# A gated recurrent layer on one core: six product groups of 64 columns become five, one of them 128 columns wide

## The reference

```python
def step(h, x_t):
    fused = sigmoid(concatenate([x_t, h], axis=-1) @ w_W + w_b)      # 1024 -> 1024
    hidden_state, output_state = split(fused, 2, axis=-1)            # r and z below
    memory_state = x_t @ wx_W + wx_b + hidden_state * (h @ wh_W + wh_b)
    h_new = output_state * h + (1.0 - output_state) * tanh(memory_state)
    return h_new, h_new
out = x + swapaxes(scan(step, h0, swapaxes(x, 0, 1))[1], 0, 1)
```

## Time and profile before

| | |
|---|---|
| time, median of 3 runs | 1796.21 us (1795.36 to 1796.39) |
| the profiled execution | 1795.32 us, of which its span is 1793.5 us |
| PE busy | 1766.1 us, 98% of the span |
| PEld busy | 1694.7 us, 94% |
| DVE busy | 1131.5 us, 63% |
| ACT busy | 789.8 us, 44% |
| POOL busy | 357.1 us, 20% |
| DMA | 29.9% of the 16 engines' span, mean 89 GB/s |

### The profile page before, as it was taken

How to read it: one execution, slowest core, us unless ns; L and a number is a source line. 1 busy time by engine, 2 the same in 40 slices (tenths; PEclk the granted TensorE clock), 3 DMA queues, 4 the chain that set the end, 5 groups by cost and what they waited for, 6 DMA issues and landing times.

```text
span 1793.5 us, 244402 instructions
## 1 busy us (share of the span) xinstructions
PE 1766.1 (98%) x110976; PEld 1694.7 (94%) x110976; DVE 1131.5 (63%) x7177; ACT 789.8 (44%) x3983; POOL 357.1 (20%) x1540
## 2 busy tenths in 40 slices
PE   6999999999999999999999999999999999999998
PEld 5899999999999999999999999999999999999997
DVE  2566666666666666666666666666666666666665
ACT  2444444444444444444444444444444444444443
POOL 0122222222222222222222222222222222222221
PEclk9999999999999999999999999999999999999999
DMA  6223332233332233322233322333222333223332
GB/s 215 59 87 92 92 92 76 75 92 94 93 91 72 79 92 92 93 76 81 87 92 92 92 70 80 96 92 92 82 75 85 93 95 93 73 78 91 92 92 82
DMA packets 180732, 159.89 MB, mean 89 GB/s; under 512 B 12016, under 2 KB 179440, under 8 KB 180720
## 3 DMA queue, kind: packets, MB, share of 16 engines
q1 hardware_dynamic: 180720, 159.72, 29.9%
HBM read 151.28 MB, written 8.39 MB: 89 GB/s over the span
## 4 chain that ended last, share of the span: by engine, by line
PE 97%; DMA 1%; SPq 1%; issue 0%; DVE 0%; ACT 0%; POOL 0%; POOLq 0%; DVEq 0%
PE ps L239 79%; PE ps L200 19%; DMA x_next<-in_x 1%; DMA x_sb<-in_x 0%; SPq L149 0%; SPq L158 0%; SPq L155 0%; DVE h L365 0%; SPq L146 0%; ACT h L304 0%; ACT h_by L299 0%; SPq L162 0%; SPq L153 0%; SPq L152 0%; SPq L151 0%
## 5 line engine op out<-in xcount | busy, mean ns | idle before, releaser
L239 PE MATMUL ps<-wh,h 128*8 128x64 f32 x98304 | 1504.4, 219 | 9.0 <-issue 5.1
L239 PEld LDWEIGHTS ps<-wh,h 128*8 128x8 f32 x98304 | 1390.9, 90 | 78.7 <-issue 6.7
L343 DVE STREAM_TRANSPOSE turned<-ps 128x64 f32<-128x64 f32 x3072 | 705.3, 239 | 402.6 <-PE ps L239 309.1
L295 ACT ACTIVATE m_by<-pre_r 128x16 f32<-128x16 f32 x1024 | 223.2, 218 | 548.5 <-DVE pre_r L346 548.4
L200 PE MATMUL ps<-x_next,wx_step 128*32 128x128 f32 x12288 | 430.2, 273 | 1.1 <-issue 1.1
L365 DVE TENSOR_TENSOR_SCAN h<-h_by,h 128x48 f32<-128x48 f32 x1024 | 264.0, 258 | 245.0 <-ACT h_by L299 192.1
L424 POOL TENSOR_TENSOR add<-turned,bias_h 128x16 f32<-128x16 f32 x1024 | 222.8, 218 | 714.8 <-DVE turned L343 684.3
L304 ACT ACTIVATE h<-m_pre 128x32 f32<-128x32 f32 x1024 | 237.7, 232 | 205.2 <-DVE m_pre L356 205.2
L299 ACT ACTIVATE h_by<-pre_z 128x16 f32<-128x16 f32 x1024 | 222.4, 217 | 220.6 <-DVE pre_z L350 220.6
L200 PEld LDWEIGHTS ps<-x_next,wx_step 128*32 128x32 f32 x12288 | 316.5, 110 | 1.4 <-issue 1.3
L437 POOL TENSOR_TENSOR y<-x_sb,h 128x32 f32 x512 | 134.1, 262 | 714.2 <-DVE h L365 714.2
(11 more groups left out here) (8 smaller groups left out, 1.1 us busy)
## 6 DMA issues: line engine op xcount, KB each, us to landing
wx_step<-in_w_x SPq DMA_DIRECT2D x516, 192.0 KB, 2.4
x_next<-in_x SPq DMA_DIRECT2D x132, 256.0 KB, 3.2
x_sb<-in_x SPq DMA_DIRECT2D x34, 256.0 KB, 3.2
out_h<-y SPq DMA_DIRECT2D x32, 256.0 KB, 2.7
...
bias_x<-in_b_x SPq DMA_DIRECT2D x1, 6.0 KB, 3.2
bias_h<-in_b_h SPq DMA_DIRECT2D x1, 2.0 KB, 3.0
```

The costliest lines, as they stand in the source:

```text
L239: mm = pe.matmul(ps[Q * j:Q * j + B, bank, 0:GROUP], h_of(s - 1, k), wh[:, k, j, at:at + GROUP], start=(start and k % HC == 0), stop=(not ...
L295: act.activation(m_by[:, o, :, 1], pre_r[:, o, :], ACT.Sigmoid).then_inc(r_ready[o], 1)
L343: return dve.transpose(turned[:, o, g], ps[:, GATES * o + g, 0:GROUP].rearrange("p (c q) -> p c q", q=Q))
```

## The change

Half B's R and M become one group, RM_B, of 128 columns in one bank. Its weights lie side by side already (R_B's 64 columns, then M_B's), so no array moves. A group is now a tuple of first column, number of columns and bank, and there are five: R_A, M_A, Z_A, RM_B, Z_B.

```diff
@@ constants
-    GROUP_BANKS = HALVES * GATES
-    X_BANKS = [GROUP_BANKS, GROUP_BANKS + 1, GROUP_BANKS]
+    R_A = (0, GROUP, 0)
+    M_A = (GROUP, GROUP, 1)
+    Z_A = (2 * GROUP, GROUP, 2)
+    RM_B = (3 * GROUP, 2 * GROUP, 3)
+    Z_B = (5 * GROUP, GROUP, 4)
+    GROUP_BANKS = 5
+    X_BANKS = [5, 6, 7]
@@ PE, x products
-                        if u == 0:
-                            pe.wait_ge(xg_free[2], free)
-                        elif u == 1:
-                            pe.wait_ge(xg_free[1], free)
-                        else:
-                            pe.wait_ge(xg_free[0], again)
+                        pe.wait_ge(xg_free[u], free)
@@ PE, h products
-            def products(o, g, half, s, start):
-                bank = GATES * o + g
-                at = GROUP * bank
+            def products(group, half, s, start):
+                at, cols, bank = group
                 for k in range(half * HC, (half + 1) * HC):
                     for j in range(TILES):
-                        mm = pe.matmul(ps[Q * j:Q * j + B, bank, 0:GROUP], h_of(s - 1, k),
-                                       wh[:, k, j, at:at + GROUP], start=(start and k % HC == 0),
+                        mm = pe.matmul(ps[Q * j:Q * j + B, bank, 0:cols], h_of(s - 1, k),
+                                       wh[:, k, j, at:at + cols], start=(start and k % HC == 0),
                                        stop=(not start and k % HC == HC - 1), tile_position=(0, Q * j))
@@ PE, step
                 pe.wait_ge(h_ready[0], nxt)
-                products(0, R, 0, s, True)
-                products(0, M, 0, s, True)
-                products(0, Z, 0, s, True)
-                products(1, M, 0, s, True)
+                products(RM_B, 0, s, True)
+                products(R_A, 0, s, True)
+                products(M_A, 0, s, True)
+                products(Z_A, 0, s, True)
                 pe.wait_ge(h_ready[1], nxt)
-                products(0, R, 1, s, False).then_inc(r_done[0], 1)
-                products(0, M, 1, s, False).then_inc(m_done[0], 1)
-                products(0, Z, 1, s, False).then_inc(z_done[0], 1)
-                products(1, R, 0, s, True)
-                products(1, R, 1, s, False).then_inc(r_done[1], 1)
-                products(1, M, 1, s, False).then_inc(m_done[1], 1)
-                products(1, Z, 0, s, True)
-                products(1, Z, 1, s, False).then_inc(z_done[1], 1)
+                products(R_A, 1, s, False).then_inc(r_a_done, 1)
+                products(M_A, 1, s, False).then_inc(m_a_done, 1)
+                products(Z_A, 1, s, False).then_inc(z_a_done, 1)
+                products(RM_B, 1, s, False).then_inc(rm_b_done, 1)
+                products(Z_B, 0, s, True)
+                products(Z_B, 1, s, False).then_inc(z_b_done, 1)
@@ ACT, step
                 reset(1, nxt)
+                update(1, nxt)
                 new(1, s, nxt)
-                update(1, nxt)
@@ DVE, turn
-            def turn(o, g):
-                return dve.transpose(turned[:, o, g], ps[:, GATES * o + g, 0:GROUP].rearrange("p (c q) -> p c q", q=Q))
+            def turn(group, o, g0, g1):
+                at, cols, bank = group
+                return dve.transpose(turned[:, o, g0:g1].rearrange("p g c q -> p (g c) q"),
+                                     ps[:, bank, 0:cols].rearrange("p (c q) -> p c q", q=Q))
@@ DVE, step, behind sum_r(0); what stands there in full is shown below
-                turn(1, R).then_inc(r_turned[1], 1)
-                turn(1, M).then_inc(m_turned[1], 1)
+                turn(RM_B, 1, R, Z).then_inc(rm_b_turned, 1)
@@ POOL, hidden
-                pool.wait_ge(m_turned[o], nxt)
+                pool.wait_ge(rm_b_turned if o else m_a_turned, nxt)
```

More of the change, by code:

```diff
@@ L110, in build @@
         constants = sem("constants")
-        r_done = halves("r_done")
-        m_done = halves("m_done")
-        z_done = halves("z_done")
-        r_turned = halves("r_turned")
-        m_turned = halves("m_turned")
-        z_turned = halves("z_turned")
+        r_a_done = sem("r_a_done")
+        m_a_done = sem("m_a_done")
+        z_a_done = sem("z_a_done")
+        rm_b_done = sem("rm_b_done")
+        z_b_done = sem("z_b_done")
+        r_a_turned = sem("r_a_turned")
+        m_a_turned = sem("m_a_turned")
+        z_a_turned = sem("z_a_turned")
+        rm_b_turned = sem("rm_b_turned")
+        z_b_turned = sem("z_b_turned")
         x_product = sem("x_product")
@@ L207, in first_x_products @@
                 for u, k in x_list:
-                    if k == 0 and u >= X_UNITS - 1:
-                        last = max(v for v in range(u) if X_BANKS[v % X_UNITS] == X_BANKS[u % X_UNITS])
-                        pe.wait_ge(xg_free[last % X_UNITS], last // X_UNITS + 1)
+                    if k == 0 and u >= X_UNITS:
+                        pe.wait_ge(xg_free[u % X_UNITS], u // X_UNITS)
                     if k == 0 and u * WX_PARTS % UNITS == 0:
@@ L213, in first_x_products, with x_products @@
                     x_product_of(u, k, wx[:, u, k, :], x_sb[:, k, 0:TOK])
-            def x_products(loaded, free, again, s):
+            def x_products(loaded, free, s):
                 pe.wait_ge(wx_step_loaded[s], loaded)
@@ L277, in _ @@
                     step(i, t0, s)
-                    x_products(loaded, free, again, s)
+                    x_products(loaded, free, s)
         @block.scalar
@@ L371, in step @@
                 par = s % 2
-                dve.wait_ge(r_done[0], nxt)
+                dve.wait_ge(r_a_done, nxt)
                 if s % RING == 0:
                     dve.wait_ge(y_added, held(dve, t0 + (s + STEPS)))
-                turn(0, R).then_inc(r_turned[0], 1)
-                dve.wait_ge(m_done[0], nxt)
-                turn(0, M).then_inc(m_turned[0], 1)
+                turn(R_A, 0, R, M).then_inc(r_a_turned, 1)
+                dve.wait_ge(m_a_done, nxt)
+                turn(M_A, 0, M, Z).then_inc(m_a_turned, 1)
                 dve.wait_ge(x_placed, nxt)
-                dve.wait_ge(r_turned[0], nxt)
+                dve.wait_ge(r_a_turned, nxt)
                 sum_r(0, par, nxt)
-                dve.wait_ge(z_done[0], nxt)
-                turn(0, Z).then_inc(z_turned[0], 1)
-                dve.wait_ge(r_done[1], nxt)
-                turn(1, R).then_inc(r_turned[1], 1)
-                dve.wait_ge(z_turned[0], nxt)
+                dve.wait_ge(z_a_done, nxt)
+                turn(Z_A, 0, Z, GATES).then_inc(z_a_turned, 1)
+                dve.wait_ge(z_a_turned, nxt)
                 sum_z(0, par, nxt)
                 mix_m(0, par, nxt)
-                dve.wait_ge(m_done[1], nxt)
-                turn(1, M).then_inc(m_turned[1], 1)
-                dve.wait_ge(r_turned[1], nxt)
+                dve.wait_ge(rm_b_done, nxt)
+                turn(RM_B, 1, R, Z).then_inc(rm_b_turned, 1)
+                mix_h(0, s, nxt)
+                dve.wait_ge(rm_b_turned, nxt)
                 sum_r(1, par, nxt)
-                mix_h(0, s, nxt)
-                dve.wait_ge(z_done[1], nxt)
-                turn(1, Z).then_inc(z_turned[1], 1)
+                dve.wait_ge(z_b_done, nxt)
+                turn(Z_B, 1, Z, GATES).then_inc(z_b_turned, 1)
+                dve.wait_ge(z_b_turned, nxt)
+                sum_z(1, par, nxt)
                 mix_m(1, par, nxt)
-                dve.wait_ge(z_turned[1], nxt)
-                sum_z(1, par, nxt)
                 mix_h(1, s, nxt)
```

5 lines of the change are left out of this document (2 added, 3 removed).

## The result

| | before | after |
|---|---|---|
| median | 1796.3 us | 1778.62 us (1777.43 to 1780.79, 4 runs) |
| ratio | | 0.9904, 95% interval 0.9887 to 0.9921 |
| profiled execution, span | 1795.32, 1793.5 us | 1779.06, 1777.2 us |
| step in the stage 300 to 1700 us | 3.415 us | 3.390 us |

The change gains 17.7 us. I had forecast 1751 us and a range of 1746 to 1775: the direction is right, but only two fifths of the gain came, and the time lies outside the range.

The account below looks back on a forecast made before the run. PE was taken as the bound, with one late start a step: 3.415 - 0.021 (fewer passes) - 0.068 (late start) = 3.326 us a step; 512 x 0.089 = 45.4 us, so 1796.21 becomes 1751, 8-in-10 range 1746 to 1775.

Parts of the forecast that it names:

- What bounds it: PE's own time sets the end; its one break, at the wait for `h_ready[1]`, costs 0.068 us a step.
- Part 1: On PE, 16 passes of 64 columns become 8 of 128, saving 0.021 us a step, 10.6 us in all.
- Part 2: More PE work ahead of `h_ready[1]` gives half B 0.213 us more, removing the 0.068 lateness: 34.8 us.
- part 3: Chains behind PE on DVE, ACT and POOL: both states arrive in time, with 0.03 (half A) and 0.02 us (half B) spare.
- deadline of 2.15: Half A's state must be written by 2.15 us after the first pass behind `h_ready[1]`; forecast at 2.12.
- the joint turn: RM_B's single turn on DVE ahead of half A's `mix_h`: may hold DVE 0.38 us, bounds 0.17 to 0.34, costs nothing.
- rival 1: State late again by 0.02 to 0.07 us: 1761 to 1786, likeliest near 1764; sign: PEld idle behind `mix_h`; chance 0.36.
- The swap of tanh and sigmoid: Half B's changed order on ACT costs nothing, as both are ready at nearly the same time.
- keeps its time: The kernel's first step is set by loads, so its time does not change.
- Rival 2: The wait at `h_ready[1]` itself costs, so the 0.068 us stays: 1785.6 us; chance 0.06.
- rival 3: The wide turn blocks DVE, delaying half A's `mix_h`; slower from a 0.51 us hold, 1848 at 0.60; chance 0.03.
- rival 4: A wide PE pass is much cheaper than the x pass, its cost mostly fixed: 1736 to 1746 us; chance 0.03.

Follow-up runs that it names:

- part 2 alone: The kernel before with only R_B's chunks 0 and 1 moved ahead of PE's wait for half B's state: 1761.90 us.
- the fastest kernel: The changed kernel with the joint turn cut in two, M_B's first, and the output-add wait moved to M_A's turn, counted from 1: 1749.00 us.

## Why the prediction was wrong

**What bounds it: right.** PE, with one late start at `h_ready[1]`. The 0.068 us and its 34.8 us were confirmed by the run with part 2 alone (33.7).

**Part 1: right.** A wide pass costs what the x pass costs; 0.020 us a step measured, 0.021 forecast.

**Part 2: right by itself**, and in the change eaten up again, by part 3.

**Part 3 is the step that failed, at one link.** Up to the tanh of half A the chain holds: counted from the first pass behind `h_ready[1]` I had M_A's turn at 0.70 and `mix_h` at 1.86, which is 1.16 apart; in after the first two turns end at 1001.68 and a turn takes 0.25, so M_A's starts at 1001.43, and `mix_h` at 1002.61: 1.18. But "`mix_h` 1.86 to 2.12" took 0.32 us, to 2.18, past the deadline of 2.15. I had costed the joint turn only by how long it holds DVE, and never followed what it releases: it ends at 1.48 + 0.29 = 1.77, POOL's add of half B follows at 0.08, that is 1.85, and `mix_h` at 1.86. I never worked out the 1.85, so I didn't see that it is `mix_h`'s own start. The trace of before had the same pair 0.08 apart, with `mix_h` at 1002.70, and no loss:

```profile
1002.62 0.22 POOL L424 TENSOR_TENSOR add<-turned,bias_h 128x16 f32<-128x16 f32 x1 [0.79 <-DVE turned L343]
```

So the rows gave no price; but they did show the two engines at work at nearly the same moment, and I should have asked for one. The sign that I had named for rival 1 is there too: weight loads idle behind `mix_h`, now at `h_ready[0]`.

The price is 26 us, more than half of what was to be had: the step falls from 3.387 to 3.337 when the add is moved (from `mix_h` to `mix_h`), 0.050 x 512 = 26, and the times from 1778.6 to 1752.8. It is about as large as the 0.057 us itself, since half A passes it on to PE at `h_ready[0]`, and half B, queued behind `mix_h` on DVE, at `h_ready[1]`; what one has cost already, the other need not pay again.

**The slack was the true risk.** I had 0.02 and 0.03 us to spare, and the range of 1775 stood for some 0.05 us of lateness. Rival 1 (0.36) is what happened in effect, "the state is late again", but with the mechanism missing: 1778.6 lies inside its 1761 to 1786, far from the 1764 that I had as likeliest, and outside the range of 8 in 10, which I had cut through that rival. With the collision gone, the sum comes out within 2 us by the medians (1752.8 against 1751), and that is in part luck: its step is 3.337 and not 3.326, nearly 6 us too much, of which the wait for the output adds, a term that I had left out, is 4, and the start of the kernel, which the sum had at nothing, gave some back. By the profiled execution, 1754.40 against 1749.9, it is 4.5 off.

**Small ones.** "The swap of tanh and sigmoid costs nothing" missed the point: taken out of the fastest kernel, with DVE's new order kept, it turns the gain into a loss of 44 us against before. That the first step "keeps its time" is about right, but the first four together are 2.8 us shorter in after than in before; whether by the third x bank or by the fewer passes stays open. The output add's wait I left out; it costs 4 us in after. Rival 2 (the wait itself costs) fell with the part 2 run, rival 3 (the joint turn blocks DVE) with its 0.292 us, and rival 4 with the 0.020.
